# A Mamba-style scan with attention, eight batches: the next batch's front and first jobs placed inside the scans

## The reference

```python
xz = einsum('bchw,oc->bohw', x, in_proj_w)            # x: normalised, 96 -> 2*192 channels
xx, z = split(xz, 2, axis=1); z1 = gelu(z)
xx = gelu(depthwise_conv3x3(xx, conv_w) + conv_b)
xs = stack([x_hw, x_wh, reversed x_hw, reversed x_wh])  # K = 4 directions of length L
x_dbl = einsum('bkdl,kcd->bkcl', xs, x_proj_w)        # 12 rows dt, 16 rows B, 16 rows C
delta = softplus(einsum('bkrl,kdr->bkdl', dts, dt_w) + dt_b)
h = h * exp(delta * A) + (delta * u) * B              # scan over L, 4*192 channels x 16 states
y = einsum('bkdn,bkn->bkd', h, C) + u * Dskip
# the four directions are summed, layer norm over 192 channels, times z1, out_proj, + residual
qkv = depthwise_conv3x3(conv1x1(gn(x)))               # 8 heads of 12
attn = softmax(normalise(q) @ normalise(k).T * SCALE); out = proj(attn @ v)   # 2304 x 2304 per head
```

## Time and profile before

| | us |
|---|---|
| median of three runs | 11197.91 |
| the profiled execution | 11183.75 |
| its span, first to last instruction | 11181.9 |
| VectorE busy | 8288.1 (74%) |
| TensorE busy | 7561.9 (68%) |
| GpSimd busy | 6348.7 (57%) |
| ScalarE busy | 6339.2 (57%) |
| mean granted TensorE clock | 0.783 |

### The profile page before, as it was taken

One profiled execution on the slowest core, in us unless ns is written; L12 is line 12 of the kernel. 1 busy time (PEld: TensorE's weight loads), 2 busy tenths in 40 slices (PEclk: granted clock), 3 DMA queues, 4 the chain that ended last, 5 costly groups with the idle time before them and its releaser, 6 DMA issues.

```text
span 11181.9 us, 192632 instructions
## 1 busy us (share of the span) xinstructions
PE 7561.9 (68%) x53104; PEld 2446.8 (22%) x53104; DVE 8288.1 (74%) x11547; ACT 6339.2 (57%) x11827; POOL 6348.7 (57%) x4028
## 2 busy tenths in 40 slices
PE   4665478873788638885488845887458873788758
PEld 1221122221222212221122211222112221222212
DVE  4998668865889658896599955998669876689630
ACT  3332357743677437773377734776357753677468
POOL 3785447744677337764278633875347744577320
PEclk7555579975899759996599956998579985899779
DMA  3554145531555225551355513555135541455310
GB/s 90 179 178 147 24 143 180 176 106 32 165 184 172 77 56 172 184 165 53 81 176 186 160 35 102 177 181 155 30 116 177 183 129 25 147 182 175 101 23 19
DMA packets 686795, 1410.24 MB, mean 126 GB/s; under 512 B 74400, under 2 KB 334272, under 8 KB 678080
## 3 DMA queue, kind: packets, MB, share of 16 engines
q1 hardware_dynamic: 686016, 1401.21, 41.2%
HBM read 1186.22 MB, written 214.70 MB: 125 GB/s over the span
## 4 chain that ended last, share of the span: by engine, by line
issue 49%; POOL 18%; PE 14%; DVE 8%; DMA 5%; ACT 4%; SPq 1%; POOLq 1%; DVEq 0%; ACTq 0%
POOL hc_buf L692 9%; PE ps L1369 3%; PE ps L1399 2%; PE ps L1400 2%; DMA rep<-bc_scratch 2%; PE ps L1222 2%; DVE ps L996 2%; DVE job_buf L1020 1%; POOL job_buf L309 1%; DVE rings L1020 1%; POOL job_buf L330 1%; ACT probs_buf L796 1%; POOL job_buf L337 1%; DMA hc_buf<-y_scratch 1%; PE ps L1441 1%
## 5 line engine op out<-in xcount | busy, mean ns | idle before, releaser
L796 ACT ACTIVATE probs_buf<-ps 128x384 f32<-128x384 f32 x6912 | 3071.2, 497 | 1738.8 <-PE ps L1288 1719.8
L692 POOL TENSOR_TENSOR hc_buf<-rings,rep 128x768 f32<-128x768 f32 x1152 | 2095.0, 1819 | 2257.1 <-DVE rings L1020 2253.0
L996 DVE TENSOR_TENSOR ps<-ps,rep 128x384 f32<-128x384 f32 x4608 | 2534.6, 551 | 620.9 <-PE ps L1197 420.4
L1197 PE MATMUL ps<-st_buf,pick_channel 96*128 96x384 bf16 x4608 | 1676.4, 364 | 1217.1 <-DVE rings L1020 713.6
L692 POOL TENSOR_TENSOR hc_buf<-job_buf,rep 128x768 f32<-128x768 f32 x1152 | 2094.3, 1818 | 523.3 <-DVE job_buf L1020 509.4
L1288 PE MATMUL ps<-qp_buf,kp_buf 108*128 108x384 bf16 (+1 forms) x6912 | 2172.2, 344 | 115.7 <-ACT job_buf L766 47.5
L1222 PE MATMUL ps<-probs_buf,v_buf 128*13 128x384 f32 x13824 | 1541.0, 520 | 31.8 <-ACT probs_buf L796 17.9
L1210 PE MATMUL ps<-hc_buf,sum_states 128*32 128x144 f32 x24576 | 1451.3, 322 | 111.8 <-POOL hc_buf L692 111.8
L787 ACT ACTIVATE st_buf<-st_buf,a_cols 128x768 f32<-128x768 f32 x1152 | 1080.6, 938 | 283.9 <-DMA st_buf<-delta_scratch 280.5
L787 ACT ACTIVATE rings<-rings,a_cols 128x768 f32<-128x768 f32 x1152 | 1078.2, 937 | 185.6 <-DMA rings<-delta_scratch 185.6
L1288 PEld LDWEIGHTS ps<-qp_buf,kp_buf 108*128 108x128 bf16 x6912 | 659.8, 98 | 2113.3 <-ACT probs_buf L796 973.7
(11 more groups left out here) (161 smaller groups left out, 9530.7 us busy)
## 6 DMA issues: line engine op xcount, KB each, us to landing
st_buf<-delta_scratch SPq DMA_DIRECT2D x1152, 384.0 KB
rings<-delta_scratch SPq DMA_DIRECT2D x1152, 384.0 KB
part_scratch<-job_buf SPq DMA_DIRECT2D x1152, 72.0 KB, 2.1
st_buf<-part_scratch SPq DMA_DIRECT2D x192, 432.0 KB, 7.0
rep<-bc_scratch SPq DMA_DIRECT2D x192, 384.0 KB
delta_scratch<-job_buf SPq DMA_DIRECT2D x192, 192.0 KB, 4.8
qp_buf<-qk_scratch SPq DMA_DIRECT2D x864, 36.0 KB
kp_buf<-qk_scratch SPq DMA_DIRECT2D x432, 72.0 KB
```

The lines of the kernel that those rows point to most:

```text
L692: pool.tensor_tensor(hc[tile % 2][:, chunk(kk, v)], h_ring[t % 2], rep_third(1, kk, v), ALU.mult).then_inc(s["hc_ready"], 1)
L796: act.activation(probs[(m % 2) * HG + h], bank(slots["score", p]), ACT.Exp, scale=SCALE)\
L996: dve.tensor_tensor(bu, bu, rep_piece(0, kk, v), ALU.mult)\
L1197: pe.matmul(bank(BANK_U[x % 3]), pick(x // 2), st[x // 2 // SPG][:, piece(v)], start=True, stop=True)\
```

## The change

The front of batch b + 1 is cut into nine stretches of steps and placed in the first nine stretches of the directions of batch b (`front_step` on every engine). Stretch 0 normalises: statistics on VectorE, the rest on GpSimd; x stays in DRAM as `xn_scratch`. Stretches 1 to 6 take one chunk of 8 rows each: input projection with a halo of one row on either side, ScalarE's copy into a padded buffer, the convolution as nine matmuls with diagonal weights for each of two channel groups, Gelu, the even half of x_proj, stores of u and of the projected rows to DRAM; GpSimd and ScalarE write the transposed u. Stretches 7 and 8 make the odd half of x_proj from the transposed u. All of this uses one PSUM bank, number 2, which is taken from the ring of scores. A Gelu brings a load of its table, and `preload_act_table_set` loads the exp and ln table again. For batch 0 the same steps run by themselves (`start`), and so do its nine first jobs, on ScalarE and VectorE as before.

The fourth direction now holds the first jobs of the next batch. All jobs read u and dt from DRAM copies that SP loads four steps ahead (`load_job`), and the stores of delta and parts stand six and eleven steps after the job's start; job 2's parts are stored in the next stretch. Between back and scan only `enter` is left: rep, deltas, parts, and then queries and keys. In `back` u is loaded from DRAM beside y. `stretches` writes out all three stretches. Queries have two buffers instead of three, the parts of k lie in `y_acc`, and the first evacuation of y waits until they are stored. At a change of direction the second part load stands ahead of the rep loads. The diff, cut to its core:

```diff
-JOB_START = (1, 7, 13)
-ACT_STAGES = {"abs": 0, "relu": 0, "exp": 1, "ln": 2}
-POOL_STAGES = {"add": 4, "times_u": 5, "u0": 6, "u_rest": 7, "u1": 8, "u2": 9}
+LOAD_JOB = (0, 5, 11)
+JOB_START = (4, 9, 15)
+ACT_STAGES = {"abs": 0, "relu": 0, "exp": 1, "ln": 1}
+POOL_STAGES = {"add": 3, "times_u": 4, "u0": 5, "u_rest": 6, "u1": 7, "u2": 8}
 ACT_JOBS = sorted((JOB_START[j] + t, j, i, n) for j in range(JOBS) for i, (n, t) in enumerate(ACT_STAGES.items()))
...
-SCAN_RING = 3
+SCAN_RING = 2
...
-        def batches(engine, front, directions, back, attention):
-            front(0)
-            directions(0, None)
+        def batches(engine, start, enter, directions, back, attention):
+            start()
+            enter(0)
+            directions(0, None, True)
             back(0)
-            if NB > 1:
-                with engine.Fori(1, NB) as b:
-                    front(b)
-                    directions(b, b - 1)
-                    back(b)
+            with engine.Fori(1, NB - 1) as b:
+                enter(b)
+                directions(b, b - 1, True)
+                back(b)
+            enter(NB - 1)
+            directions(NB - 1, NB - 2, False)
+            back(NB - 1)
             attention(NB - 1)
         def stretches(engine, body):
-            body(0, True)
-            with engine.Fori(1, NS) as q:
-                body(q, False)
+            for q in range(NS):
+                with engine.Fori(0, 1):
+                    body(q, q == 0)
...
+                    apart(sp)
+                    sp.wait_ge(s["dt_mm"], BI * JOBS + 2)
+                apart(sp)
+                u_src, d_src = of_batch(u_dram, b)[0, k % 2], of_batch(xd_dram, b)[0, k % 2]
+                r = DT_ROWS[k]
+                if j < 2:
+                    cols = piece(2 * q + j)
+                    sp.dma_start(job_d[:, piece(j)], d_src[r:r + R, cols]).then_inc(job_loaded[j], 16)
+                    sp.dma_start(job_u[:, piece(j)], u_src[0:DA, cols]).then_inc(job_loaded[j], 16)
+                else:
+                    for hf in range(2):
+                        cols = slice(hf * HL + q * PC, hf * HL + (q + 1) * PC)
+                        sp.dma_start(job_d[:, piece(hf)], d_src[r:r + R, cols]).then_inc(job_loaded[j], 16)
+                        sp.dma_start(job_u[64 * hf:64 * hf + 64, 0:PC], u_src[DA:DI, cols])\
+                          .then_inc(job_loaded[j], 16)
...
+                prep = same or more
                 last = q + 1 == NS
...
+                elif same:
+                    sp.wait_ge(s["ubc"], (kidx + 1) * (2 * DSTEPS))
+                    load_st(kk + 1, 1)
                     for c in range(1, SPT):
                         sp.wait_ge(s["hc_ready"], (kidx + 1) * DSTEPS - (SPT - c))
-                        load_rep(kk + 1, c)
-                    sp.wait_ge(s["ubc"], (kidx + 1) * (2 * DSTEPS))
-                    apart(sp)
-                    sp.wait_ge(part_stored[0], (kidx + 2) * NS * 128)
-                    load_st(kk + 1, 1)
+                        load_rep(b, kk + 1, c)
+                elif more:
...
+            def enter(b):
                 later = not (isinstance(b, int) and b == 0)
                 if later:
-                    sp.wait_ge(s["n_mul"], b * NORMS)
+                    store_parts(b - 1)
+                    sp.wait_ge(s["v_ev"], b * 5)
                     apart(sp)
-                sp.dma_start(xin, a["x"][bass.ds(b, 1), :, :].rearrange("b c l -> (b c) l"))\
-                  .then_inc(s["x_loaded"], 16)
-                if later:
-                    store_parts(b - 1)
-                    first_queries_keys()
-                sp.wait_ge(s["xn_ready"], b * 2 + 1)
-                apart(sp)
-                sp.dma_start(xn_dram, xn).then_inc(s["xn_stored"], 16)
-                sp.wait_ge(s["xd_ev"], (b + 1) * NPC)
-                apart(sp)
-                sp.dma_start(bc_dram, bc_stage).then_inc(s["bc_stored"], 16)
-                sp.wait_ge(s["bc_stored"], 16 * (b + 1))
-                apart(sp)
                 for i in range(SPT):
-                    load_rep(0, i)
-                for q in range(NS):
-                    for j in range(JOBS):
-                        store_delta(b, 0, q, j)
-                        store_job(b, 0, q, j)
+                    load_rep(b, 0, i)
                 for n in range(LEAD):
                     first_deltas(b * K, 0, n)
                 sp.wait_ge(part_stored[0], (b * K + 1) * NS * 128)
@@ -600,15 +712,20 @@
                 apart(sp)
                 for g in range(2):
                     load_st(0, g)
-            def directions(b, ab):
+                if later:
...
@@ -632,11 +749,16 @@
                     p = slice(64 * hf, 64 * hf + 64)
                     sp.dma_start(y[1][p, :], y_dram[0, DA:DI, hf * HL:(hf + 1) * HL]).then_inc(s["y_loaded"], 16)
                     sp.dma_start(yt[1][p, :], y_dram[1, DA:DI, :]).then_inc(s["y_loaded"], 16)
+                    sp.dma_start(u[1][p, :], of_batch(u_dram, b)[0, 0, DA:DI, hf * HL:(hf + 1) * HL])\
+                      .then_inc(s["y_loaded"], 16)
+                sp.dma_start(u[0], of_batch(u_dram, b)[0, 0, 0:DA, :]).then_inc(s["y_loaded"], 16)
...
+                            apart(act)
+                        p = (128, 64)[i]
+                        dst = pads[i][:, :].rearrange("p (h w) -> p h w", w=PADW)[:, :, 1:1 + W]
+                        act.copy(dst, square(ps[0:p, BANK_F, 0:XC])).then_inc(s["f_pad"], 1)
+                    if t == 13:
+                        act.wait_ge(s["f_conv"], 2 * n + 1)
+                        apart(act)
+                        at_least(act, "f_us", 32 * n)
+                        apart(act)
+                        at_least(act, "f_ut", 2 * n)
+                        apart(act)
+                        act.copy(uc[0][:, :], bank(BANK_F)).then_inc(s["f_pre"], 1)
+                    if t == 19:
+                        act.wait_ge(s["f_conv"], 2 * n + 2)
+                        apart(act)
+                        act.wait_ge(s["f_pre"], n + 1)
+                        apart(act)
+                        act.activation(uc[1][:, :], bank(BANK_F, 64), ACT.Gelu, bias=conv_bias[1][0:64, :])\
+                            .then_inc(s["f_gelu"], 1)
...
+                elif f <= CHUNKS:
+                    c, n = f - 1, fb * CHUNKS + f - 1
+                    if t == 4:
+                        pe.wait_ge(s["f_chunk"], (n + 1) * 16)
+                        if c in (0, CHUNKS - 1):
+                            pe.wait_ge(s["f_edge"], fb * 2 + (1 if c == 0 else 2))
+                        if c == 0:
+                            pe.wait_ge(s["f_std"], (fb + 1) * 2)
+                        else:
+                            pe.wait_ge(s["f_xd"], fb * 12 + c)
+                        pe.matmul(bank(BANK_F, n=XC), in_proj[:, 0:DA], xc[:, :], start=True, stop=True)\
+                          .then_inc(s["f_in"], 1)
+                    if t == 6:
+                        pe.wait_ge(s["f_pad"], 2 * n + 1)
+                        pe.matmul(bank(BANK_F, 64, XC), in_proj[:, DA:DI], xc[:, :], start=True, stop=True)\
+                          .then_inc(s["f_in"], 1)
+                    if 8 <= t < 13:
+                        if t == 8:
+                            pe.wait_ge(s["f_pad"], 2 * n + 2)
+                        conv_taps(0, 2 * (t - 8))
+                    if 14 <= t < 19:
+                        if t == 14:
+                            pe.wait_ge(s["f_pre"], n + 1)
+                            apart(pe)
+                        conv_taps(1, 2 * (t - 14))
+                    if t == 21:
+                        pe.wait_ge(s["f_gelu"], 2 * n + 2)
+                        pe.matmul(bank(BANK_F), x_proj[0][:, 0:128], uc[0][:, :], start=True, stop=False)
+                        pe.matmul(bank(BANK_F), x_proj[1][0:64, 0:128], uc[1][:, :], start=False, stop=True)\
+                          .then_inc(s["f_xp"], 1)
+                else:
+                    for i in range(3):
+                        if t == 6 + 6 * i:
...
+            def conv_taps(i, tap0):
+                p = (128, 64)[i]
+                for tap in range(tap0, min(tap0 + 2, 9)):
+                    ins = pe.matmul(square(bank(BANK_F, p)), conv_w[i][:, tap * p:(tap + 1) * p],
+                                    window(pads[i][:, :], tap, 8), start=(tap == 0), stop=(tap == 8))
+                    if tap == 8:
+                        ins.then_inc(s["f_conv"], 1)
```

More of the change, by code:

```diff
@@ L728, in back @@
                 apart(pool)
-            batches(pool, front, directions, back, attention)
+            batches(pool, start, lambda b: None, directions, back, attention)
         @block.scalar
@@ L1338, in stretch @@
                         score(PER_STEP * t + 2)
+                    if scan and more and kk * NS + q < FRONT:
+                        front_step(b + 1, kk * NS + q, t)
             def last_leftover(ab):
@@ L1467, in attention @@
```

(4 more changed lines are left out.)

588 lines of the change are left out of this document (380 added, 208 removed).

## The result

The changed kernel takes 11582.85 us in the median of four runs (11557.58 to 11603.47), the kernel before, run with it, 11188.12 (11176.61 to 11211.42): ratio 1.0349, 95% interval 1.0319 to 1.0379. That is 3.5% slower, where I had forecast 1.3% faster; it lies outside my range and on the side of rival B.

What follows compares the result with a forecast made beforehand. VectorE, busy 74% of 11181.9 us, was taken to set the scans' pace, with fronts outside them. -1030 + 630 + 24 + 28 + 56 + 150 = -142 gave 11042 for the profiled execution, 11055 as median; range 10650 to 11330.

Steps and rivals of the forecast that it cites:

- rival B: Two score banks couple the queues too tightly: 7 us instead of 2 in 84 stretches, 11475 us; chance 0.18.
- Step 1: Between back and scan: seven fronts leave the serial path, 51 of 198 us stay each, -1030 us.
- Rival C: The entry takes the front's place on SP's queue: 85 us instead of 51, 11295 us; chance 0.10.
- Step 2: TensorE's front work in the scans: 11.5 us per chunk stretch, 4.3 in stretch 0, 2.5 each in 7 and 8.
- The sentence on the Trainium skill: About 2.66 us per ScalarE table switch with a drain: up to 100 us more over 36 chunk stretches, about 11150.
- Step 3: Two score banks instead of three: 2 us in each of 84 stretches with attention, ends 0 and 5.5.
- Step 4: Jobs in the fourth direction: +1 us in each of three stretches; operand loads from DRAM cost nothing.
- Step 5: Sum per pass: 105 us, six passes +630; last pass +24 for the ring; first pass +28, ends 10 and 120.
- Step 6: In back, u is read from DRAM ahead of y_summed: 7 us, eight times, +56.
- Step 7: The first front runs as a serial chain: 371 us instead of 215, +150, range 80 to 240.
- My signs for B: Stretches without front work passing 75 us would show the two score banks couple the queues too tightly.
- A (TensorE has room): A chunk costs 7 us and no bank or table is felt: -566, 10630 us; chance 0.22.

Runs made afterwards that it cites:

- a_combo: Changed kernel with job, denominator and projection products behind the third score of their step, and a third score bank in stretches without front work: 11189 us.
- b_both: Kernel before with two score banks instead of three and jobs at steps 4, 9, 13 instead of 1, 7, 13: 12052.84 us, ratio 1.0767.
- b_jobs4: Kernel before with jobs at steps 4, 9, 13 instead of 1, 7, 13, three score banks kept: 11701.08 us, ratio 1.0454.
- a_joblast: Changed kernel with job, denominator and projection products behind the third score of their step, two score banks kept: 370 us less than the changed kernel.
- c_onetap: a_combo with one of nine convolution taps per channel group, the others left out: 10792.08 us, 397 less than a_combo.
- b_jobs3: Kernel before with jobs at steps 3, 8, 13 instead of 1, 7, 13, three score banks kept: 11548.3 us, ratio 1.0322.
- c_job3: a_combo with the first job at step 3 instead of 4: 11237.86 us, ratio 1.0044 to the kernel before.
- c_split: a_combo with one tap of each pair moved from the end of its step to its middle: 11232.81 us, ratio 1.0041 to the kernel before.
- c_notable: a_combo with Abs in place of Gelu in the front's steps, so no table loads between them: 11011.83 us, 177 less than a_combo.
- b_joblast: Kernel before with job, denominator and projection products behind the third score of their step: 0.9% faster than the kernel before.

## Why the prediction was wrong, by its own steps

**Step 1, the entry.** Right: 316.7 us for seven, 45 each, where I had 51, inside 35 to 80. Rival C (85) is out: loads went at 186 GB/s where I took 174. Of the 8 us that I had added for loads queued behind the keys, a part stands in stretch 0 instead: there VectorE waits 2.5 us for x and TensorE 3.6 for a job's operand (3038 to 3124 us).

**Step 2, the chunk.** The mechanism was right, the size was not. a_combo's stretches in batches 1 to 6, from first scan to first scan, are on average 16.0 us longer than before's in a chunk stretch (11.5 forecast), 16.1 in stretch 0 (4.3), 6.8 in stretches 7 and 8 (2.5). Tables: 4.2 on the path instead of 2 and a part of 1 for hand-offs; I had let half a step of lead swallow 1.6 us, and the trace shows TensorE at a stand of 2.87 us behind the loads. Taps: 6.6 for eight of nine, so some 7.4 for all, against about 7: right. What was too small is the rest, some 4.4 by difference where I had left 1.5 for projection and x_proj: step 4 takes 5.1 and is not light, as I had it, since a job stands in it, and step 6 takes 3.9. In stretch 0 I costed GpSimd's normalisation at 3 of 1.8 us beside other work; it is 2.92 each, ahead of the products that free VectorE's ring, and steps 17 and 18 take 5.6 and 5.1, 5.1 us more than before. The statistics and their wait for x add 5.3 in steps 3 to 6, and the small operations 2.7 in step 10:

```profile
3093.66 2.92 POOL L784 TENSOR_SCALAR ut_a<-ut_a,f_gn 96x768 f32<-96x768 f32 x1
```

I had taken the duration from a row of another operation and its cover from the idle time of a stretch.
The sentence on the Trainium skill (ScalarE: Activation LUTs, What ACT_TABLE_LOAD costs; 2.66 us for a switch) gave 100 us more. Two such switches are 5.3, and steps 19 to 21 get 5.2 shorter without them, the stretch 4.2. In the rows, though, a load is 1.28, begins 0.02 after the last exp and ends 0.01 before the next operation; no drain is to be seen, and what adds to the loads is TensorE's stand behind them. The measured 4.2 lies between my 3 and the page's 5.3; the page's reason, the drain, isn't shown here.

**Step 3, the score banks.** One of the two steps that each turn the sign, and the one whose mechanism was mispriced. The price of two banks alone was somewhat low (2.8 measured, 3.9 by b_both against b_jobs4; 2 forecast, ends 0 to 5.5). The change also moves the jobs from steps 1, 7, 13 to 4, 9, 15, and I priced the banks on a job that ScalarE reads right behind one exp, with the bank free after some 2.1 us; ScalarE reads it behind the third score of the step, which TensorE issues after the job, and the bank is held 3.4 us. Together they cost 380 us in batches 1 to 7 (after less a_combo, 309 + 71; 340 against a_joblast), where I had 168. That is 4.5 in each of 84 stretches, 5.9 in those of the last batch; my worst sum was 4.4. It was to decide from 1.7 above my 2, and it is 2.5 above. Rival B had this mechanism and this place with 7 in every stretch. It is some 7 in the last batch's stretches with jobs (75.9 against 68.7 in the table) and 7.2 to 10.5 in the last three stretches of batches 1 to 6, and only 2.2 in the chunk stretches (93.7 against 91.4 as a whole), whose steps are full anyway.

**Step 4, jobs in the fourth direction, operands by DRAM.** +1 each forecast; a_combo shows stretch 9 at 77.6 (before 79.9) and 10 and 11 within 0.5: nothing. Operands do come late in two places where I had put nothing: in stretch 0, behind the x load (TensorE waits 2.3 us once in a_combo, 3.6 in the kernel after), and in the first batch, five times, 8.4 us together.

**Step 5.** Six passes +1053 instead of +630: 309 of it the coupling by a_combo (144 forecast), the remaining 744, 124 a pass, step 2's three sizes with step 4's small term (486 forecast). Last pass +69, the coupling alone: a_combo has -2. First pass +99 instead of +28, inside 10 to 120: 13 us a chunk. Of these 3.2 are in step 4 (5.9 instead of 2.7), where a job and the input projection meet. For the taps I had supposed that after a burst the clock stays up. It does for the first channel group and not for the second (TensorE's timeline, first batch):

```profile
511.29 1.46 PE L1453 MATMUL ps<-pad_a,conv_w_a 128*128 128x384 f32 x4
...
519.92 2.82 PE L1453 MATMUL ps<-pad_b,conv_w_b 64*64 64x384 f32 x4
```

From the last tap of the first group to 517.90 TensorE only broadcasts, 0.34 us in each 1.3; from there its products are the longer ones (broadcasts 0.50), and four taps take 2.82 instead of 1.46, the step 6.2 us.

**Step 6, back.** +57 for +56. The wait for the loads is 35.3 us each (282.6/8; 28.7 in the earlier trace rows):

```profile
  DMA rep<-u_scratch: 282.6, 8
```

**Step 7, the first front.** 397 instead of 371: c_onetap takes 85 us from it with eight of nine taps, 14 a chunk.

**Rivals and range.** From forecast to result, 530 us of span: the coupling 210 more than forecast, the sizes of step 2 in batches 1 to 6 258, the first pass 71, the first front 32, the entry 43 less. From -142 each of the first two turns the sign by itself, so the forecast failed on both: the coupling of step 3 and the sizes of step 2. My signs for B were met: stretches without front work passed 75 (78), chunk stretches took 88 to 90 instead of 84, TensorE 81.6 busy instead of 75, and VectorE's waits in one (3125 to 3215 us) are well over 12:

```profile
DVE ps L1207 <- PE ps L1468: 18.9, 19, 2.6
```

A (TensorE has room) is out. B has the mechanism and half of its price; 0.18 was too little for it, as it turned out, and a range that left its centre out did not hold both misses together. I had written that a blocked score holds the broadcasts behind it, and had not looked in ScalarE's timeline at where it reads a job against the third score.

b_jobs3's step 3 is dearer than a_combo's step 4 (4.1 against 3.0) with three banks in both, and its order differs too. c_job3 parts them in the last batch, where it has a_combo's order, three banks and no front: steps 3 and 4 take 4.0 and 2.7, together 6.7, against 2.9 and 3.0 in a_combo and 4.1 and 3.6 in b_jobs3. So 0.8 of the 1.8 us is the place and 1.0 the order. The score behind the job does not wait there (TensorE's timeline of c_job3); why step 3 takes a job worse than step 4 is argued only, from TensorE's having no idle time there behind the denominators:

```profile
9801.77 0.91 PE L1509 MATMUL ps<-job_d,dt_proj_a 12*128 12x384 f32 x2
9802.61 0.34 PE L1467 MATMUL ps<-st_buf,pick_channel 96*128 96x384 bf16 x1
9802.78 0.49 PE L1557 MATMUL ps<-qp_buf,kp_buf 108*128 108x384 bf16 x2
```

What stays open: where the some 40 us of c_split and c_job3 come from, and what share of the coupling is the lower clock that comes with it (below).

## What to carry to other kernels

Where two engines hand buffers of a small ring to each other, give both the same order inside a step: a product that is issued early and read late cost as much here as a missing bank (54 and 52 us in the last batch), and either cure left little for the other. On an engine that is 87% busy, don't count its idle time as free: of 12 us of taps, 6.6 came back when they were left out, though 8.8 us of the stretch had been idle. Take the duration of each moved operation from a row with its own shape. When one edit shrinks a ring and another moves what is lent from it, price them together.

## What the runs showed of the hardware

A pair of table loads of 1.28 us each cost 4.2 us in a chunk stretch beside attention, where TensorE waits for what ScalarE does between them, and nothing in the first batch, where it does not (c_notable).

TensorE's clock fell to its lower level in stretches of the kernel after where it stayed up in the kernel before. In the stretch above TensorE waits 1.57 us for the denominator, and its next scores take 0.50 us instead of 0.34:

```profile
9997.87 0.34 PE L1558 MATMUL ps<-qp_buf,kp_buf 108*128 108x384 bf16 x1
...
10000.03 1.62 PE L1499 MATMUL ps<-att_buf,pick_den 128*128 128x384 f32 x2 [1.57 <-DVE att_buf L1249]
...
10002.99 0.50 PE L1558 MATMUL ps<-qp_buf,kp_buf 108*128 108x384 bf16 x1
```

The wait alone does not explain it. The kernel before has the same wait at the same place, and its scores stay at 0.34:

```profile
9682.26 0.88 PE L1228 MATMUL ps<-att_buf,pick_den 128*128 128x384 f32 x2 [1.57 <-DVE att_buf L1035]
...
9683.84 0.34 PE L1288 MATMUL ps<-qp_buf,kp_buf 108*128 x1
```

The granted clock of such a stretch is 1.00 in the kernel before (9676 to 9747 us, 71 us long) and in b_joblast (68), 0.89 in the kernel after (78) and 0.93 in a_combo (9680 to 9751, 71):

```profile
9585.00:9653.00 68.00, 59.26 (x530) 19.33 (x528) 67.15 (x105) 56.23 (x111) 58.01 (x44) 1.00 0.57 184
```

a_combo is as short as the kernel before at a lower clock, so the clock is not all of the 7 us; no run parts its share.
